# A gated four-part kernel: Silu of two linear steps as (1 + tanh(g/2)) times half the gated value, with new instruction orders

## What is computed

```python
# 1: two int8-style linears; smooth factors from column maxima, integers from row maxima
def _smooth_quant_linear(x, w):
    amax_x = jnp.max(jnp.abs(x), axis=0); amax_w = jnp.max(jnp.abs(w), axis=0)
    s = jnp.maximum(jnp.sqrt(jnp.maximum(amax_x, EPS) / jnp.maximum(amax_w, EPS)), EPS)
    xs, ws = x / s, w * s
    x_scale = jnp.maximum(jnp.max(jnp.abs(xs), axis=-1, keepdims=True), EPS) / QMAX
    w_scale = jnp.maximum(jnp.max(jnp.abs(ws), axis=-1, keepdims=True), EPS) / QMAX
    x_q = jnp.clip(jnp.round(xs / x_scale), -QMAX, QMAX)
    w_q = jnp.clip(jnp.round(ws / w_scale), -QMAX, QMAX)
    return x_q @ w_q.T * x_scale * w_scale.T
def _expert_forward(xe, guw, dw):            # per batch: guw = fside (512x512), dw = ctx (512x256)
    gate, up = jnp.split(_smooth_quant_linear(xe, guw), 2, axis=-1)
    return _smooth_quant_linear(jax.nn.silu(gate) * up, dw)
# 2: ternary-weight gated feed-forward, gate_w and val_w 2048x512, out_w 512x2048
bit_linear(silu(bit_linear(x, gate_w, gate_b)) * bit_linear(x, val_w, val_b), out_w, out_b)
# 3: x @ softmax((ctx Wq + bq)(ctx Wk + bk)^T)^T, per batch
# 4: a mixture of 8 small experts, the best 2 of each row
```

## Time and profile before

| | |
|---|---|
| median of three runs | 468.16 us (467.05 to 469.64) |
| the profiled execution | 470.15 us, its span 468.4 us, mean granted TensorE clock 0.978 |
| busy, share of the span | PE 90%, DVE 81%, ACT 75%, POOL 47% |
| instructions | PE 2183, DVE 955, ACT 574, POOL 343 |
| front, before the tile steps are in full run | about the first 207 us |

### The profile page before, as it was taken

The page is one execution under the profiler, slowest core; times in us unless marked ns, Lnnn a source line. Parts: engine busy times, 40 slices in busy tenths (PEclk is TensorE's granted clock), DMA queues, the critical chain, the costliest instruction groups (busy, mean ns, idle before and its releaser), DMA issues.

```text
span 468.4 us, 7366 instructions
## 1 busy us (share of the span) xinstructions
PE 419.6 (90%) x2183; PEld 245.0 (52%) x2183; DVE 380.8 (81%) x955; ACT 351.1 (75%) x574; POOL 221.6 (47%) x343
## 2 busy tenths in 40 slices
PE   4747879988988987789999999999999999999986
PEld 3736756746745543345455545545545554554563
DVE  3787687989987889377898898889889889888853
ACT  1397798876799989857887787778788778777532
POOL 3276761688796764644343333333424333441220
PEclk9957998999999999999999999999999999999999
DMA  8999668553474701511221331231223123122101
GB/s 303 388 343 302 125 228 177 198 162 68 73 244 90 228 10 23 91 23 33 47 49 42 68 60 42 63 75 38 54 68 46 46 67 60 47 65 67 45 25 45
DMA packets 84936, 49.53 MB, mean 106 GB/s; under 512 B 70936, under 2 KB 73496, under 8 KB 83872
## 3 DMA queue, kind: packets, MB, share of 16 engines
q1 hardware_dynamic: 84896, 49.06, 39.9%
HBM read 28.33 MB, written 4.19 MB: 69 GB/s over the span
## 4 chain that ended last, share of the span: by engine, by line
PE 63%; DVE 10%; ACT 7%; DMA 6%; POOL 6%; issue 5%; SPq 2%; ACTq 0%; DVEq 0%; POOLq 0%
PE p_out L1895 11%; PE p_out L1807 11%; PE p_val L1800 11%; PE p_gate L1800 11%; PE p_tr L1782 3%; DMA att_t<-in_L_ffn_val_w 3%; PE p_out L1829 3%; PE p_out L1855 3%; DMA att_t<-in_L_ffn_gate_w 2%; PE p_tr L1685 2%; ACT val_t L1268 2%; POOL w_slots L529 2%; DVE h_max L775 1%; ACT o_q L1285 1%; PE p_val L1751 1%
## 5 line engine op out<-in xcount | busy, mean ns | idle before, releaser
L1800 PE MATMUL p_gate<-gate_t,q_room 128*128 128x512 fp8e4 x256 | 65.7, 379 | 2.5 <-ACT p_gate L1400 2.5
L1800 PE MATMUL p_val<-val_t,q_room 128*128 128x512 fp8e4 x256 | 65.7, 379 | 0.2 <-ACT p_val L1410 0.2
L1807 PE MATMUL p_out<-att_t,qT_room 128*128 128x512 f32 x120 | 55.4, 603 | 0.9 <-ACT qT_room L1230 0.9
L1895 PE MATMUL p_out<-out_t,ws_f 128*128 128x512 fp8e4 x240 | 54.4, 379 | 1.5 <-DMA ws_f<-ws_f 1.5
L597 POOL TENSOR_TENSOR rstd<-mv,ln_eps 128x1 f32<-128x1 f32 x48 | 9.2, 192 | 94.2 <-DVE mv L866 87.1
L1400 ACT ACTIVATE p_gate<-w_slots,seed_scale 128x512 f32<-128x512 f32 x64 | 43.6, 684 | 11.2 <-POOL seed_scale L618 9.8
L1385 ACT ACTIVATE ctx_sb<-p_gate,bcol 128x512 f32<-128x512 f32 x64 | 43.8, 684 | 9.8 <-issue 4.5
L895 DVE TENSOR_TENSOR act_f<-p_val,ctx_sb 128x512 f32<-128x512 f32 x64 | 44.1, 689 | 6.8 <-PE p_val L1800 5.4
L897 DVE TENSOR_REDUCE mu<-act_f 128x1 f32<-128x512 f32 x64 | 43.9, 686 | 2.2
L1410 ACT ACTIVATE p_val<-w_in,seed_scale 128x512 f32<-128x512 f32 x64 | 43.6, 682 | 0.0
L1800 PEld LDWEIGHTS p_gate<-gate_t,q_room 128*128 128x128 f16 x256 | 24.9, 98 | 31.5 <-issue 8.6
(11 more groups left out here) (242 smaller groups left out, 988.8 us busy)
## 6 DMA issues: line engine op xcount, KB each, us to landing
att_t<-in_L_ffn_out_w SPq DMA_DIRECT2D x6, 1024.0 KB, 5.0
w_in<-in_fside_BxS2xS SPq DMA_DIRECT2D x4, 1024.0 KB, 6.9
att_t<-in_L_ffn_gate_w SPq DMA_DIRECT2D x4, 1024.0 KB, 13.0
att_t<-in_L_ffn_val_w SPq DMA_DIRECT2D x4, 1024.0 KB, 9.4
out_dram<-x_all SPq DMA_DIRECT2D x15, 256.0 KB, 2.3
x_all<-in_x SPq DMA_DIRECT2D x2, 1024.0 KB, 11.2
x_all<-in_x SPq DMA_DIRECT2D x1, 2048.0 KB, 17.3
ctx_sb<-in_ctx SPq DMA_DIRECT2D x4, 512.0 KB, 6.2
```

Of the source, the lines that this page charges most:

```text
L1800: last = nc.tensor.matmul(bank[:, c % 2, :], x_t[n % 2][:, k * P:(k + 1) * P], w_t[m][:, k, cols], start=False, stop=k == KD - 1, skip_gro ...
L1807: last = nc.tensor.matmul(p_out[:, 0, :], lt_c[:, k * P:(k + 1) * P], att_t[:, bass.ds((n // T) * (KD * S) + k * S, S)], start=k == 0, sto ...
L1895: last = nc.tensor.matmul(p_out[:, 0, :], p_t[:, k * P:(k + 1) * P], w_t[2][:, k, :], start=k == 0, stop=k == KH - 1)
```

## The change

1. **Silu.** With half the value in the second half of `h_hs`, Silu(g) v is (1 + tanh(g/2)) g (v/2). ACT now evaluates `Tanh` with scale 0.5. POOL's `h_gated` multiplies the gate half by the value half as soon as they are dequantised, without waiting for ACT. A new DVE instruction, the new `h_hidden`, adds 1 to the tanh and multiplies. The half comes from `scale` of the weights' second half, multiplied by 0.5 in an added small DVE instruction.
2. **Small operations.** In `ratio`, `smooth` and `row_scales` the small `tensor_scalar` and `tensor_tensor` are written as `scalar_tensor_tensor`; one of them takes `step_share`, a constant tile.
3. **First rows.** Batch 0 of x is loaded in four transfers of 256 KB in place of one of 1 MB, and each tile's statistics wait for their own.
4. **Orders.** The lists of the front are rearranged on all engines. `tanh_gates` moves to the opening, and on SP `fside_load(1)` and the small loads now stand ahead of `val_load(2)` and `val_load(3)`.

```diff
-                def h_hidden(b, t):
-                    pool.wait_ge(a_silu, T * b + t + 1)
+                def h_gated(b, t):
+
+                    pool.wait_ge(a_mm_used[0], T * b + t + 1)
                     if t == 0:
                         need(pool, a_q16[1], T * (2 * b - 1))
...
-                    nc.gpsimd.tensor_tensor(a_f[:, t * C:(t + 1) * C], gate_s[:, t % 2, :], h_hs[:, t % 2, C:2 * C],
-                                            ALU.mult).then_inc(a_hidden, 1)
+                    nc.gpsimd.tensor_tensor(a_f[:, t * C:(t + 1) * C], h_hs[:, t % 2, 0:C], h_hs[:, t % 2, C:2 * C],
+                                            ALU.mult).then_inc(a_gated, 1)
...
+                def h_hidden(b, t):
+
+                    dve.wait_ge(a_silu, T * b + t + 1)
+                    dve.wait_ge(a_gated, T * b + t + 1)
+                    nc.vector.scalar_tensor_tensor(a_f[:, t * C:(t + 1) * C], gate_s[:, t % 2, :], 1.0, a_f[:, t * C:(t + 1) * C],
+                                                   ALU.add, ALU.mult).then_inc(a_hidden, 1)
...
-                    nc.scalar.activation(gate_s[:, t % 2, :], h_hs[:, t % 2, 0:C], ACT.Silu).then_inc(a_silu, 1)
+                    nc.scalar.activation(gate_s[:, t % 2, :], h_hs[:, t % 2, 0:C], ACT.Tanh, scale=0.5).then_inc(a_silu, 1)
...
-                    link(nc.vector.tensor_scalar(scale[z][:, r, :], rowmax[z][:, r, :], QUANT_EPS, 1.0 / (QMAX * STEP), ALU.max, ALU.mult))
-                    nc.vector.reciprocal(qscale[z][:, r, :], scale[z][:, r, :]).then_inc(a_qscale[z], 1)
+                    link(nc.vector.scalar_tensor_tensor(scale[z][:, r, :], rowmax[z][:, r, :], QUANT_EPS, step_share[:, :], ALU.max, ALU.mult))
+                    if z == 0 and r == 1:
+                        link(nc.vector.reciprocal(qscale[z][:, r, :], scale[z][:, r, :]))
+                        nc.vector.tensor_scalar(scale[z][:, r, T // 2:T], scale[z][:, r, T // 2:T], 0.5, None, ALU.mult).then_inc(a_qscale[z], 1)
+                    else:
+                        nc.vector.reciprocal(qscale[z][:, r, :], scale[z][:, r, :]).then_inc(a_qscale[z], 1)
...
-                x_load(0, 0)
+                first_x_load()
                 fside_load(0)
+                w_load(0, 2)
                 w_load(0, 0)
-                w_load(0, 2)
                 w_load(0, 3)
                 w_load(0, 1)
+                x_load(1, 1)
                 x_load(2, slice(2, NB))
-                x_load(1, 1)
+                val_load(1)
                 val_load(0)
-                val_load(2)
-                val_load(1)
-                val_load(3)
                 fside_load(1)
                 small_loads()
+                val_load(2)
+                val_load(3)
                 integers(0, 0, 0)
                 integers(0, 0, 1)
```

More of the change, by code:

```diff
@@ L259, in flamingo_gated_kernel @@
         chunk_loaded = [sem(f"chunk_loaded{c}") for c in range(4)]
-        x_loaded = [sem(f"x_loaded{n}") for n in range(3)]
+        first_x_loaded = [sem(f"first_x_loaded{t}") for t in range(T)]
+        x_loaded = [sem(f"x_loaded{n}") for n in range(1, 3)]
         fside_loaded = sem("fside_loaded")
@@ L377, in out_load_again, with first_x_load @@
                     w_load(2, c)
+                def first_x_load():
+                    for t in range(T):
+                        sp.dma_start(xs[:, 0, t], xv[:, 0, t]).then_inc(first_x_loaded[t], 16)
                 def x_load(n, batches):
-                    sp.dma_start(xs[:, batches], xv[:, batches]).then_inc(x_loaded[n], 16)
+                    sp.dma_start(xs[:, batches], xv[:, batches]).then_inc(x_loaded[n - 1], 16)
                 def small_loads():
@@ L472, in _ @@
                 out_load_again(0)
+                integers(0, 3, 0)
+                out_load_again(1)
+                integers(0, 3, 1)
                 ctx_load(3)
[L474 to L478, removed]
                 val_b_load()
                 x_transpose(0)
+                gate_b_load()
                 integers(1, 2, 0)
                 integers(1, 2, 1)
+                out_b_load()
                 x_transpose(1)
@@ L1068, in _ @@
                 ratio(0, 1)
+                w_mean(1)
                 smooth(0, 1)
+                h_statistics(3)
+                h_scaled_act(1)
                 h_dequantise(0, 0)
                 h_dequantise(0, 1)
-                h_scaled_act(1)
+                h_hidden(0, 0)
+                h_hidden(0, 1)
                 h_dequantise(0, 2)
@@ L1140, in _ @@
                 h_scaled_act(3)
-                q_statistics(0)
+                h_hidden(2, 0)
+                h_hidden(2, 1)
                 h_dequantise(2, 2)
@@ L1144, in _ @@
                 row_scales(0, 3, 0)
+                row_scales(0, 3, 1)
+                o_dequantise(1, 0)
                 t_maximum(2, 0)
+                o_dequantise(1, 1)
                 t_maximum(2, 1)
-                o_dequantise(1, 0)
-                o_dequantise(1, 1)
-                row_scales(0, 3, 1)
+                o_dequantise(1, 2)
                 t_reciprocal(2, 0)
+                h_hidden(2, 2)
+                q_statistics(0)
+                o_dequantise(1, 3)
+                h_hidden(2, 3)
                 o_context_max(2)
-                o_dequantise(1, 2)
-                o_dequantise(1, 3)
                 column_max(1, 2, 0, 0)
@@ L1179, in _ @@
                 o_dequantise(2, 3)
[L1180 removed]
+                h_hidden(3, 3)
+                link0(b_product(0, 1))
                 column_max(1, 3, 0, 0)
[L1182 removed]
+                link0(b_product(0, 2))
                 column_max(1, 3, 0, 1)
                 ratio(1, 3)
[L1185 removed]
+                link0(b_product(0, 3))
                 smooth(1, 3)
[L1187 removed]
                 b_quantise(0, link0)
@@ L1507, in _ @@
                 rounded(1, 1, 0)
-                rounded(1, 1, 1)
+                scale_row(1, 1)
                 h_silu(2, 0)
@@ L1978, in _ @@
                 t_energies(0, 2)
-                columns(0, 2, 0, 2)
-                columns(0, 2, 0, 3)
                 t_energies(0, 3)
+                scale_row(0, 1)
                 products(0, 1, 0)
                 products(0, 1, 1)
+                rows(0, 2)
                 products(0, 1, 2)
+                products(0, 1, 3)
                 t_transpose(0, 2)
                 t_transpose(0, 3)
-                rows(0, 2)
-                t_context(1)
-                products(0, 1, 3)
-                t_query_key(1)
                 scale_row(1, 0)
```

409 lines of the change are left out of this document (212 added, 197 removed).

## The result

The changed kernel takes 475.65 us (median of 4; 475.09 to 479.54) against 468.84 for the kernel before in the same comparison: a ratio of 1.0178, 95% interval 1.0138 to 1.0217. It is **slower**, outside the range that I gave (451.5 to 469). The profiled execution has a span of 473.3 us against 468.4.

A forecast was written before the change was run, and what follows sets the result against it. PE bounds the tile steps, so gains come from the first 207 us: weights, then DVE densest, then ACT. Terms -4.1 + 0 - 3.85 = -7.95 on the median 468.16 give 460.2, stated as 460.5, range 451.5 to 469.

The forecast's parts named there:

- The last term: 130 to 207 us: ACT, the bound for the first 30 us, sheds 3 table loads: -3.85, bounds 0 and -6.6.
- rival C: Front: all table loads and POOL products count in full, 15.8 less, giving 452.5; chance 0.20.
- The middle term: 60 to 130 us: DVE's new work +1.4, one ACT load on the chain -1.3: 0, bounds -6.4 and +3.8.
- rival B: From 60 us on: DVE's new h_hidden waits for POOL, 6.6 us over 16, giving +5, 465.5; chance 0.16.
- The opening: Up to the first products: they begin at 53.5 against 57.57, last val sum at 45: -4.1, bounds -7 and +1.
- Rival D: Opening: late val loads, last val sum starting at 49 instead of 45, make it slower, 473; chance 0.08.

The follow-up runs named there:

- tables_gone: The kernel before with ACT evaluating tanh(g/2) in place of Silu and nothing else changed: 469.71 us, ratio 1.0031.
- silu_new_orders: The changed kernel with the Silu back, POOL's product behind it, and the 16 new DVE instructions and the halving gone; new orders kept: 478.86 us.
- hidden_reduce: The changed kernel with each of the 16 new DVE instructions replaced by a maximum over the same tanh tile, waits and queue place kept: 470.52 us.
- opening_old: The changed kernel with the lists of all five engines as before up to the first dequantisations, four transfers kept: 475.07 us.
- small_alone: The kernel before with only the small operations of ratio, smooth and row_scales in the three-operand form: 467.95 us, ratio 0.9978.
- first_rows: The kernel before with only the four transfers of batch 0: 468.75 us, ratio 1.0017.

## Why the prediction was wrong, point by point

**The last term failed: -3.85 from 130 us on, "and it is the bound for the first 30 us".** I took ACT's 29.36 of 30 us for a bound. It was full, but the end did not hang on it: the chain ran over POOL and PE, and ACT's loads filled time in which it would have waited. tables_gone shows that the loads cost nothing in the old orders: -0.5 us in the middle, nothing in the time. That POOL's list held that stretch instead is read from the chain and the windows; no run made POOL's work shorter. The count of three was right for the changed kernel: its loads at 170.76, 200.23 and 215.15 answer to those at 169.70, 192.46 and 197.10 before.

**A term was missing: the new orders behind the opening.** I gave them nothing of their own, and rival C even a gain. With the Silu the new orders as a whole cost 10.8 us (silu_new_orders, 478.86 against 468.07): by the sections 2.4 before the first products, 1.9 in the middle and 4.1 late. In these orders the eight loads do count, with 8.1 us, so that taking them out repaid mostly what the new orders had first made of them. I took 5.1 us for loads (1.3 and 3.85) off the time of the kernel before, where they are worth nothing.

The page of the Trainium skill that I weighed, "ScalarE: Activation LUTs", section "What ACT_TABLE_LOAD costs", prices a switch higher than the 1.283 us of the rows; no run here shows a gain for either price in the old orders, and in the new ones the eight loads cost 1.0 us each, less than both.

**The middle term failed: 0, with DVE's 16 instructions at 0.44.** This was my rival B, and its conditions came true: 12.2 us, a maximum of 1.49 and a sum 5.2 above the 7.0 that I had reckoned (B said 6.6). I priced it at +5, half of 6.6 and 3.2, by the argument that only part of it stands on the path. hidden_reduce gives 5.1 us for it, all of what was stretched, so B's +5 came out by luck. B's answer, 465.5, was wrong mostly because the +5 stood on a gain of 8 that was not there: 468 + 5 is 473, and some 2.6 us remain to the measured time. The Trainium skill, "SBUF — State Buffer", section "Who interferes with whom", names the pair: a VectorE instruction with two SBUF inputs beside a GpSimd instruction that reads SBUF. The runs agree in all three kinds (two SBUF inputs up to 1.49 us, a reduction 0.42, one input in PSUM 0.43), and also in its consequence that the small operations would gain nothing.

**The opening failed: -4.1.** I set the last val sum at 45, it began at 48.90; and from its start to the first products I had 8.5 us, it took 11.0, with the clock at 0.50. The 3.9 and the 2.5 together turn -4.1 into +2.3. The issue of the two loads came as I had said (36.70, I had 37.0); the landing did not. The named reason was wrong: "nothing else is left to load ahead of the two". The eight transposes of the integers went out at 41.00 right behind the two loads, whose issue took 4.26 us, and the DMA share was 1.02 and 1.26 in the two five-us windows from 40 to 50. How much of the landing the transposes took was not tested. Rival D's point (49) was all but met and the products came 2.3 us later. But D's price was not there: with the products back at 56.67 (opening_old) 0.6 us comes back by the medians, the intervals overlapping. So the opening is no gain, and that it is part of the loss is not shown.

**Small operations and four transfers: nothing** (small_alone and first_rows), as I had costed them: 0 of the 3.2 us if the form waits, and the transfers at nothing.

**What I had named for the profile after.** ACT's busy time (341.3) and its 6 loads came as said, and so did nothing that follows from them. DVE's came at 393.2 instead of 385, the maximum of h_hidden at 1.49 (I had put 1.7 as the sign of B), the last val sum at 48.90 instead of 45, and the clock from 60 to 130 us at 0.95 instead of 0.98. PE is dense from about 212 us, not from 199. The chain that ended last has DVE for 14% of the span, 10% before.

**What the numbers add up to.** Without table loads and without new DVE work both sets of orders stand at about the same place: 469.71 (old) and 470.80 (new), with overlapping intervals. On that base, the loads cost nothing in the old orders and 8.1 us in the new; the DVE instructions without stretching cost nothing in the new orders (470.52) and about 6.5 in the old (476.18); stretching costs 5.1 in the new and 1.8, within the noise, in the old. The change is the last kind of pair: new orders, tanh, stretched. The kernel before is the one pair in which nothing of its own overhead shows in the time. The new lists hide the plain work of the tanh form; what they don't hide is DVE waiting for POOL.

Left open: why the two bases lie 0.3 and 0.6% above the kernel before, which has more work. Both intervals begin just above 1 (1.0002 and 1.0033). In tables_gone 1.4 us of it is seen once, as a TensorE clock of 0.71 from 180 to 185 us where before has 1.00, but that is one execution. None of the 16 kernels beats the kernel before by more than its interval.

## What to carry to other kernels

A busy share near 1 says that an engine is full, not that it holds the end: look whether the chain that ended last runs over it there, and price a removal by removing it alone, in the orders in which it will be made. Before moving an elementwise operation to DVE, look at where its inputs lie and what POOL does beside it; with one input in PSUM it kept its plain duration here, though the wait that this put on PE left little of the gain. Orders written by hand fit one set of durations, so a change of form and a change of order must be judged as a pair, both crosses run.

## What the runs showed of the hardware

- A DVE instruction of three operands with both inputs in SBUF (128x256) took 0.42 us alone. The seven stretched ones all began while POOL was in an elementwise product of its own; they took up to 1.49 and ended 0.28 us after that product. POOL is drawn out as well: its four pieces took 5.32 us there, 4.96 before. With one input in PSUM (0.43 at most) and as a reduction (0.42) it was not stretched beside the same POOL work.
- A 128x4 operation is hit as hard (up to 1.26 us for 0.16 to 0.17), in either form.
- After a wait of 5.0 us on PE the granted clock was 0.50 (its 1.2 GHz level) in the next 5 us, and 16 products of 128 columns took 3.62 us instead of 2.05. With products without use in that wait it was 1.00.
- The clock differs between executions of nearly the same program: `t_query_key` of batch 0 took 5.40 us in the kernel before and 3.70 in small_alone, which is 1.7 of the 2.7 us by which their middles differ.
